# Block 1's pass of a graph network on one Trainium2 core: its stores issued by another queue, part of its arithmetic on GpSimd, and the corrected sums of split nodes in a block of their own

## What is computed

```python
def block1(x, src, dst, W, b):          # 200000 pairs and 12500 loops
    msg = relu(concatenate([x[src], x[dst]], axis=-1) @ W.T + b)
    agg = segment_sum(msg, src, num_segments=12500)
    return relu(concatenate([x, agg], axis=-1) @ W.T + b)

h = maximum(layernorm(x), 0); x = x + block0(h, src, dst)     # 4 softmax heads over the nodes, sum over edges, elu
h = maximum(layernorm(x), 0); x = x + block1(h, src, dst)
h = maximum(layernorm(x), 0); x = x + block2(h, src, dst)     # three graph attention layers: 8, 8 and 1 heads
h = maximum(layernorm(x), 0); x = x + block3(h, edge_attr)    # a mean of messages over the edges
```

## Time and profile before

| | |
|---|---|
| median of 3 runs | 15976.06 us (15976.02 to 15996.48) |
| profiled execution | 15981.7 us, span 15980.0 us |
| busy, share of the span | TensorE 51%, VectorE 42%, ScalarE 35%, GpSimd 70% |
| phase e1, first to last copy of sums | about 5076 to 5820 us |
| phases f0 and f1 | 2399 to 2445 us and 5824 to 5870 us |

### The profile page before, as it was taken

The page is one execution under the profiler, slowest core; times in us unless marked ns, Lnnn a source line. Parts: engine busy times, 40 slices in busy tenths (PEclk is TensorE's granted clock), DMA queues, the critical chain, the costliest instruction groups (busy, mean ns, idle before and its releaser), DMA issues. The chain is left out here.

```text
span 15980.0 us, 259817 instructions
## 1 busy us (share of the span) xinstructions
PE 8190.7 (51%) x75456; PEld 7411.3 (46%) x75456; DVE 6692.7 (42%) x24144; ACT 5666.0 (35%) x13371; POOL 11257.5 (70%) x11862
## 2 busy tenths in 40 slices
PE   6555552565664763434432444432344444888886
PEld 4555441455554653333332333332344443777775
DVE  5555554777775863333335333335222224211112
ACT  2555551677774531222221222221111112333332
POOL 4777767677775457777767777776777775577776
PEclk9776765878877975666665666665555555799998
DMA  4444442222223743444432444443333332344443
GB/s 153 162 161 162 162 142 57 96 93 91 92 93 120 257 155 93 146 146 146 146 117 72 146 146 146 146 143 60 77 85 85 85 85 54 119 146 146 146 146 97
DMA packets 895395, 1965.03 MB, mean 123 GB/s; under 512 B 392230, under 2 KB 471026, under 8 KB 854067
## 3 DMA queue, kind: packets, MB, share of 16 engines
q0 software_dynamic: 361120, 582.27, 15.9%
q1 hardware_dynamic: 426179, 797.11, 14.6%
q10 hardware_dynamic: 107776, 582.40, 9.5%
HBM read 1095.74 MB, written 894.54 MB: 125 GB/s over the span
## 5 line engine op out<-in xcount | busy, mean ns | idle before, releaser
L112 POOL DMA_INDIRECT eg_got<-gat_table,eg_rows x4992 | 4714.7, 944 | 1542.1 <-issue 1512.5
L112 POOL DMA_INDIRECT e_got<-table,e_rows x3328 | 3155.6, 948 | 1031.2 <-issue 1004.6
L1321 PE MATMUL eg_ps_sum<-eg_got,eg_equal 128*128 128x136 f32 (+1 forms) x9984 | 2070.8, 382 | 280.3 <-DVE eg_got L1409 256.5
L1328 ACT ACTIVATE eg_outs<-eg_ps_sum 128x544 f32<-128x544 f32 (+1 forms) x1248 | 675.1, 541 | 4279.2 <-PE eg_ps_sum L1321 4268.9
L1321 PEld LDWEIGHTS eg_ps_sum<-eg_got,eg_equal 128*128 128x128 f32 x9984 | 1965.5, 291 | 344.2 <-ACT eg_outs L1328 189.1
L117 POOL DMA_INDIRECT sorted_rows<-sort_rows,sort_dest x1664 | 1615.9, 971 | 532.8 <-issue 495.9
L1353 PE MATMUL eg_small<-ident,eg_score 128*128 128x128 f32 (+1 forms) x312 | 138.6, 444 | 3176.1 <-DVE eg_score L1392 3176.1
L1353 PEld LDWEIGHTS eg_small<-ident,eg_score 128*128 128x128 f32 (+1 forms) x312 | 47.2, 151 | 3203.5 <-DVE eg_score L1392 3203.5
L1390 DVE TENSOR_TENSOR eg_diff<-eg_small,eg_got 128x128 f32<-128x128 f32 (+1 forms) x312 | 79.1, 253 | 2732.6 <-DMA eg_got<-gat_table,eg_rows 2732.6
L1621 DVE TENSOR_SCALAR e_got<-e_ps_second 128x512 f32<-128x512 f32 x416 | 287.6, 691 | 1758.0 <-PE e_ps_second L1604 1727.5
L567 PE MATMUL e_ps_sum<-e_got,e_equal 128*128 128x64 f32 x3328 | 628.8, 352 | 676.1 <-DMA e_got<-table,e_rows 676.1
(11 more groups left out here) (528 smaller groups left out, 20828.1 us busy)
## 6 DMA issues: line engine op xcount, KB each, us to landing
gat_out<-eg_outs ACTq DMA_DIRECT2D x208, 1152.0 KB
eg_equal_b<-equal_d SPq DMA_DIRECT2D x312, 512.0 KB
out<-e_outs ACTq DMA_DIRECT2D x208, 512.0 KB
out<-e_outs ACTq DMA_DIRECT2D x104, 1024.0 KB
values<-e_zeros_b SPq DMA_DIRECT2D x104, 768.0 KB
values_q<-e_zeros_b SPq DMA_DIRECT2D x104, 768.0 KB
sort_value<-values_q SPq DMA_DIRECT2D x104, 768.0 KB
e_value<-values SPq DMA_DIRECT2D x104, 768.0 KB
```

The source lines that it names most:

```text
L112: return e.indirect_dma_start(out, None, table, bass.IndirectOffsetOnAxis(ap=index, axis=0), **kw)
L1321: last_i = e.matmul(ps_sum[q % 2][:, i, 0:FG], equal[q % 4][:, i, :], got[k][:, t, :], start=True, stop=True)
L1328: e.activation(outs[k % 2][:, tiles, 0:FG], ps_sum[q % 2][:, :, 0:FG], ACT.Copy).then_inc(copied.sem, 1)
```

## The change

1. In e1 SP issues the stores of `out` and `last`. Its loop loads group k of the next turn, then stores group k of this turn; the first turn's loads stand ahead of the loop, the last turn's stores behind it, and `keys.load` behind those. There are four `outs` buffers instead of two.
2. In e1 the rests of odd quads go: ScalarE writes relu(rows) in fp32 to `rest` (a third activation for such a quad), GpSimd subtracts the first part from it in place. Even quads are left with VectorE. GpSimd's part stands at reach 3, before `third_part`.
3. `out` of each pass has 1664 more rows. `finish_sums` stores `patch` there in one DMA from SP. A node whose edges cross a tile has its `end_row` pointed at that block: row EP + (tile % 128) * 13 + tile / 128 for its last tile. That is worked out once at the end of e0, for both orders. `PatchRows`, `span`, `first_key`, `patch_row` and the 13 scatters of each of the six `finish_sums` are gone; `keys.load` carries one table instead of two.

The core of the diff:

```diff
@@ first_pass: VectorE's tables at the end of e0
-            e.tensor_copy(span[:, :, :, 0], pos[:, 0]).then_inc(ve, 1)
-            e.tensor_copy(span[:, :, :, 1], pos[:, 1]).then_inc(ve, 1)
+            e.tensor_scalar(tile_i[:, :, :, :], pos_i[:, :, :, :], 7, None, ALU.logical_shift_right).then_inc(ve, 1)
+            e.tensor_copy(tile_f[:, :, :, :], tile_i[:, :, :, :]).then_inc(ve, 1)
+            e.tensor_scalar(split_i[:, 0], tile_i[:, 1], P - 1, None, ALU.bitwise_and).then_inc(ve, 1)
+            e.tensor_scalar(split_i[:, 1], tile_i[:, 1], 7, None, ALU.logical_shift_right).then_inc(ve, 1)
+            e.tensor_tensor(crosses[:, :, :], tile_f[:, 0], tile_f[:, 1], ALU.not_equal).then_inc(ve, 1)
+            e.tensor_copy(split_f[:, :, :, :], split_i[:, :, :, :]).then_inc(ve, 1)
+            e.scalar_tensor_tensor(split_f[:, 0], split_f[:, 0], float(TB), split_f[:, 1], ALU.mult, ALU.add).then_inc(ve, 1)
...
+            e.scalar_tensor_tensor(split_f[:, 0], split_f[:, 0], float(EP), row_f[:, 1], ALU.add, ALU.subtract).then_inc(ve, 1)
+            e.tensor_tensor(split_f[:, 0], split_f[:, 0], crosses[:, :, :], ALU.mult).then_inc(ve, 1)
+            e.tensor_tensor(row_f[:, 1], row_f[:, 1], split_f[:, 0], ALU.add).then_inc(ve, 1)
@@ carried_pass
-        outs = [ph.sb(f"outs{k}", [P, GT, D]) for k in B2]
+        outs = [ph.sb(f"outs{k}", [P, GT, D]) for k in G4]
...
         def sync(e):
-            with e.Fori(0, TURNS) as it:
+            def load(it, k):
+                g = bass.ds(it * n4 + k, 1)
+                e.wait_ge(fills.sem, fills.at(it, (k + 1) * QUADS - U))
+                e.dma_start(value[k][:, :, :], values_v[g, :, :, :].rearrange("g p t c -> (g p) t c")).then_inc(loaded[k].sem, 16)
+                e.wait_ge(less_even.sem, less_even.at(it, ((k + 1) * QUADS - U) // 2))
+                e.wait_ge(cut_1.sem, cut_1.at(it, (k + 1) * QUADS - U))
+                e.dma_start(rows[k][:, :, :], rows_v[g, :, :, :].rearrange("g p t c -> (g p) t c")).then_inc(loaded[k].sem, 16)
+            def store(it, k):
+                g = bass.ds(it * n4 + k, 1)
+                e.wait_ge(copied.sem, copied.at(it, (k + 1) * QUADS))
+                e.dma_start(out_v[g, :, :, :].rearrange("g p t c -> (g p) t c"), outs[k][:, :, :]).then_inc(stored[k].sem, 16)
+                for a in B2:
+                    e.dma_start(ends_v[g, a, :, :], outs[k][a * (P - 1):a * (P - 1) + 1, :, :]).then_inc(stored[k].sem, 16)
+            for k in G4:
+                load(0, k)
+            with e.Fori(0, TURNS - 1) as it:
                 for k in G4:
...
+                    load(it + 1, k)
+                    store(it, k)
+            for k in G4:
+                store(TURNS - 1, k)
             keys.load(e)
+            for k in G4:
+                e.wait_ge(stored[k].sem, stored[k].at(0, TURNS))
...
-            stepped(e, (3, rests), (5, add), (7, compare))
+            stepped(e, (3, even_rests), (5, add), (7, compare))
...
             def first_part(it, q):
                 e.wait_ge(summed.sem, summed.at(it, q + 1 - CUTS))
+                if q % 2:
+                    e.wait_ge(cut_3.sem, cut_3.at(it, q + 1 - n4))
+                    e.activation(rest[q % 4][:, :, :], rows[k][:, tiles, 1:], ACT.Relu).then_inc(relued.sem, 1)
                 e.activation(cut[q % CUTS][:, 0], rows[k][:, tiles, 1:], ACT.Relu).then_inc(cut_1.sem, 1)
...
+            def odd_rests(it, q):
+                if q % 2:
+                    e.wait_ge(relued.sem, relued.at(it, q // 2 + 1))
+                    e.wait_ge(cut_1.sem, cut_1.at(it, q + 1))
+                    e.tensor_tensor(rest[q % 4][:, :, :], rest[q % 4][:, :, :], cut[q % CUTS][:, 0], ALU.subtract).then_inc(less_odd.sem, 1)
-            stepped(e, (1, third_part))
+            stepped(e, (3, odd_rests), (1, third_part))
@@ finish_sums
+            e.wait_ge(patched, 1)
+            e.dma_start(out[EP:EP + T].rearrange("(q b) c -> q b c", b=TB), patch[:, :, :]).then_inc(patch_out, 16)
+            e.wait_ge(patch_out, 16)
...
-            for b in range(TB):
-                scatter(e, out[:, :], self.patch_row[:, s, b:b + 1], patch[:, b, :], EP - 1).then_inc(patch_out, 16)
@@ Collect
-                gather(e, self.to[:, t, :], self.out[:, :], self.end_row[:, t:t + 1], EP - 1).then_inc(self.rows_in[j], 16)
+                gather(e, self.to[:, t, :], self.out[:, :], self.end_row[:, t:t + 1], EP + T - 1).then_inc(self.rows_in[j], 16)
```

More of the change, by code:

```diff
@@ L350, in first_pass @@
         pos_i = ph.sb("pos_i", [P, 2, 2, P], I32)
-        span = ph.sb("span", [P, 2, P, 2], I32)
+        tile_i = ph.sb("tile_i", [P, 2, 2, P], I32)
+        tile_f = ph.sb("tile_f", [P, 2, 2, P])
+        split_i = ph.sb("split_i", [P, 2, 2, P], I32)
+        split_f = ph.sb("split_f", [P, 2, 2, P])
+        crosses = ph.sb("crosses", [P, 2, P])
         node_rows = ph.sb("node_rows", [P, 2, 2, P], I32)
@@ L361, in first_pass @@
         group_in = ph.sem("group_in")
-        self.span = [self.dram(f"span{s}", (NP, 2), I32) for s in B2]
         row_tab = self.dram("row_tab", (2, 2, NP), I32)
@@ L1070, in carried_pass @@
         loaded = [Tally(ph, f"loaded{k}", 1, 32) for k in G4]
-        stored = [Tally(ph, f"stored{k}", 2, 48, ahead=16) for k in B2]
+        stored = [Tally(ph, f"stored{k}", 1, 48, ahead=48) for k in G4]
         spread = Tally(ph, "spread", U)
@@ L1075, in carried_pass @@
         added = Tally(ph, "added", U, ahead=2)
-        cut_1 = Tally(ph, "cut_1", U)
-        less = Tally(ph, "less", U, ahead=U)
+        cut_1 = Tally(ph, "cut_1", U, ahead=U)
+        relued = Tally(ph, "relued", U // 2)
+        less_even = Tally(ph, "less_even", U // 2, ahead=U // 2)
+        less_odd = Tally(ph, "less_odd", U // 2)
         cut_2 = Tally(ph, "cut_2", U)
@@ L1157, in add, with even_rests @@
                 e.tensor_tensor(rows[k][:, tiles, 1:], ps_fill[q % 2][:, :, 0:D], rows[k][:, tiles, 1:], ALU.add).then_inc(added.sem, 1)
-            def rests(it, q):
-                k, tiles, _ = place(q)
-                e.wait_ge(cut_1.sem, cut_1.at(it, q + 1))
-                e.wait_ge(cut_3.sem, cut_3.at(it, q + 1 - n4))
-                e.scalar_tensor_tensor(rest[q % 4][:, :, :], rows[k][:, tiles, 1:], 0.0, cut[q % CUTS][:, 0], ALU.max, ALU.subtract).then_inc(less.sem, 1)
+            def even_rests(it, q):
+                if q % 2 == 0:
+                    k, tiles, _ = place(q)
+                    e.wait_ge(cut_1.sem, cut_1.at(it, q + 1))
+                    e.wait_ge(cut_3.sem, cut_3.at(it, q + 1 - n4))
+                    e.scalar_tensor_tensor(rest[q % 4][:, :, :], rows[k][:, tiles, 1:], 0.0, cut[q % CUTS][:, 0],
+                                           ALU.max, ALU.subtract).then_inc(less_even.sem, 1)
             e.wait_ge(group_in, 16)
@@ L1745, in finish_sums @@
             ins = [(acc_t, slice(0, FO), FO)]
-            patch_rows = PatchRows(self, ph, s) if name in ("f0", "f1") else None
         F = HF if heads else FO
@@ L1878, in vector @@
             e.sem_inc(patched, 1)
-        ph.run(sync=sync, gpsimd=gpsimd, tensor=tensor, vector=vector, scalar=scalar)
+        ph.run(sync=sync, gpsimd=gpsimd if heads else None, tensor=tensor, vector=vector, scalar=scalar)
     def block0(self):
@@ L2060, in block0 @@
         self.sort()
-        out = self.dram("out0", (EP, D))
+        out = self.dram("out0", (EP + T, D))
         last = self.dram("last0", (2, T, D))
@@ L2171, in block1 @@
         values = self.values1
-        out, last = self.dram("out1", (EP, D)), self.dram("last1", (2, T, D))
+        out, last = self.dram("out1", (EP + T, D)), self.dram("last1", (2, T, D))
         self.carried_pass(values, out, last)
@@ L2231, in gat_layer @@
         FG, FO = HF + heads, HF + 2 * heads
-        out, last = self.dram(f"gat_out{n}", (EP, FO)), self.dram(f"gat_last{n}", (2, T, FO))
+        out, last = self.dram(f"gat_out{n}", (EP + T, FO)), self.dram(f"gat_last{n}", (2, T, FO))
         self.gat_pass(f"eg{n}", table, out, last, self.values2, heads, ch)
@@ L2433, in block23 @@
         ph.run(sync=sync, gpsimd=close.collect.gpsimd, tensor=tensor, vector=vector, scalar=scalar)
-        out, last = self.dram("out3", (EP, H)), self.dram("last3", (2, T, H))
+        out, last = self.dram("out3", (EP + T, H)), self.dram("last3", (2, T, H))
         self.attr_pass("e3", table, out, last, (w_attr, w_mid, b_rows, one_rows), (w_own, w_right, w_left, w_c_t, w_join, bias_e))
@@ L2873, in __init__ @@
     def __init__(self, kn, ph, s, table, dt):
-        self.first_key, self.to, self.table, self.ints = kn.first_key[s], kn.links[:, s, :], table, dt is I32
-        self.by_tile, self.last = ph.sb("key_by_tile", [NG, 2, GT], dt), ph.sb("key_last", [P, T], dt)
+        self.to, self.table, self.ints = kn.links[:, s, :], table, dt is I32
+        self.by_tile, self.last = ph.sb("key_by_tile", [NG, GT], dt), ph.sb("key_last", [P, T], dt)
```

(2 more changed lines are left out.)

126 lines of the change are left out of this document (34 added, 92 removed).

## The result

| | before | after |
|---|---|---|
| median of 4 runs each | 15976.56 us (15976.02 to 15996.48) | 15680.63 us (15680.12 to 15693.26) |
| profiled execution, its span | 15981.7, 15980.0 us | 15693.3, 15691.1 us |
| first to last copy of sums in e1 (415 quads on) | 5080.3 to 5819.9 us, 739.6 | 5054.2 to 5608.5 us, 554.3 |

The ratio is 0.9814 with the interval 0.9803 to 0.9826: 296 us less by the medians, 289 us by the two spans.

A forecast was written before the change was run, and what follows sets the result against it. No engine was full; e1 was taken to be paced by ScalarE's store issuing. Terms -181 (e1), -57 and -64 (`finish_sums`), +13.5 (key tables), +3 (e0) sum to -285.5: 15976 to 15690 us, range 15640 to 15760.

The forecast's parts named there:

- What bounds the kernel: In e1, ScalarE's issuing of three stores stops the engines together once a group, 1.53 of 7.14 us.
- Rival 3: e1 stays at 7.14 us a group because another wait replaces the stop: 15871 us, chance 0.05.
- Parts 1 to 3: e1: stores to SP, odd rests to GpSimd, DMAs become the floor; 7.14 to 5.4 us a group, 181 us saved.
- Part 2: e1: odd rests by GpSimd relieve VectorE, whose group then takes 5.0 to 5.65 us with port waits.
- Part 4: End of e1: `keys.load`, now behind the last store, comes out from under cover; +13.5 us (+10 to +16).
- Parts 5 and 6: Ends of six `finish_sums`: one store replaces 13 scatters; -57 us in f0 and f1, -64 in the four others.
- Part 7: End of e0: ten operations added to the row numbers, two casts and two DMA issues removed; +3 us.
- Rival 1: e1: GpSimd keeps the port, a waiting rest lets two queued instructions pass; 5.75 us a group, 15726 us, chance 0.22.
- Rival 2: e1: the DMA floor is softer, TensorE and VectorE hold 5.05 us a group; 15654 us, chance 0.12.
- Rival 4: e1 slower: value load waits in SP behind the store, group goes to 8.45 us; some 16020 us, chance 0.03.
- the list of what would be wrong: TensorE waiting for loads of `rows` or `value` in e1, or a store of corrected sums taking over 7 us.
- part 3: e1: the DMAs become the floor, 5.2 us a group, against 5.05 us of the engines' cadence.

The follow-up runs named there:

- e0: A phase of the kernel, not a run; ten operations on the row numbers were added at its end, measured +2.2 us.
- sp_stores: Kernel before the change, with only e1's stores moved to SP and four output buffers: 15818.12 us against 15989.31, ratio 0.9893.
- act_four_outs: Kernel before the change with four output buffers instead of two, stores still on ScalarE: 740.1 us from first to last copy in e1, against 739.6.
- odd_rests: Kernel before the change, with only the odd quads' rests moved to GpSimd and ScalarE's extra activation: 15943.18 us, ratio 0.997.
- half_value: Changed kernel loading only 8 of 16 value tiles per group after e1's first turn: 15641.2 us, ratio 0.9782 to the kernel before.
- more_loads: Changed kernel with 384 KB more loaded per group into a buffer nothing reads: 597 us from first to last copy in e1, 5.75 us a group.
- keys_early: Changed kernel with `keys.load` moved ahead of e1's pass: 3.97 us from last copy to f1's first DMA, against 12.7; first to last copy 553.4 us.

## Why the prediction was right, step by step

**What bounds the kernel: right.** The 1.53 us of issuing set the pace. sp_stores shows it by taking it away alone, act_four_outs by leaving it and changing the buffers. The sentence that VectorE's 1.26 us is the cadence between the stops is right too; odd_rests shows it, as it gains 0.45 us a group. Rival 3 is refuted by the 171 us of sp_stores. The Trainium skill (DMA: Bandwidth & Descriptors, section "Issuing engines are not separate DMA queues") calls the sequencer's time for issuing usually small beside the DMA; in this loop it was 1.53 us at the stop shown and 1.65 in the mean, of 7.13. What the prediction did not have is the clock: the echo of the stop in the kernel before includes stretches at the lower clock in 24 of 99 groups (7.44 us for 7.12), and the changed kernel has none. As an estimate from these, they are 8 of the 185 us.

**Parts 1 to 3, 5.4 us a group: right, 5.34 measured, -185.3 for -181.** But the mechanism was right only in part, and some luck is in the closeness. The two ends of the range, DMA 5.2 and VectorE waiting 5.6, were not both at work. That the transfers hold the pass is shown by half_value and by TensorE's wait for `rows`. The step "not below 5.2", a floor of full occupation, is wrong: it took a busy share of 0.98 at 348 GB/s in one burst as all that the DMA engines can do. At the 388 GB/s of more_loads the same 1808 KB would take 4.8 us, less than the engines' 4.88, and 2192 KB went in 5.75. For VectorE waiting for the port I expected half to all of 0.63 us for an even rest. Its mean over the pass, and its shortest, middle and longest duration in ns:

```profile
L1199 DVE SCALAR_TENSOR_TENSOR e_rest<-e_rows,e_cut 128x256 f32<-128x256 f32 x207 | 129.0, 623 | 32.9 <-ACT e_cut L1218 32.5
...
L1199 DVE SCALAR_TENSOR_TENSOR e_rest<-e_rows,e_cut x208: 410/611/809, 5049.5 to 5603.4; 128x256 f32<-128x256 f32 x104
```

0.62 against 0.41 undisturbed is 0.21 us, a third of it. VectorE still has 31 of 400 us idle, so little of it can have reached the end of the pass; no run takes it away. Part 2 is worth 1 to 7 of 185 us.

**Part 4: the mechanism right, the size too large.** +8.8 for +13.5, outside the +10 to +16 given. The chain took 12.7 us for 17.4. Two terms make most of it: the load by tile, which I took at 5 us between 3.3 and 7.07, is 3.24 (5609.93 to 5613.17), and the write with one issue is 1.33, not 2.9. Both were taken from rows in which the pass's own transfers ran beside them. sp_stores parts the two reasons: without those transfers a pair of loads took 4.45 instead of 7.07, and one load 3.24; a pair of writes 1.76 instead of 3.26, and one 1.33. So the company of the pass cost 2.6 and 1.5 us, and the second DMA of a pair 1.2 and 0.4. The store issues, the broadcast (4.3 for 4.8) and the change of phase are each 0.4 to 0.5 us below their terms.

**Parts 5 and 6: right.** -57.3 for -57; -66.0 for -64, as the end of an attention layer took 4.7 us for the 5.4. The bound of -102 for parts 5 and 6 together is a slip: six ends at 7.1 us instead of the 27.7 in all that the two parts use give -106. **Part 7:** +2.2 for +3; the operations on 256 elements follow each other every 0.46 us, within the 0.2 to 0.47 taken.

**Rival 1** (GpSimd keeps the port, even rests over 1.2 us) is refuted: at 5304.55 the rest got in between two queued `third_part`, and no even rest of the pass took longer than 0.81 us. **Rival 2** (the floor softer, 5.05) is refuted in its result, 75 loads in 400 us and not 79, though its idea was right: more_loads and the 407 and 422 GB/s of loads alone and the store alone show a softer floor. **Rival 4** (the value load waits behind the store) needed a landing of 14 us. The value load does stand behind the store now, and the 51st load of `rows`, issued at 5300.62, is waited for until 5308.97, 8.35 us. Of the list of what would be wrong, one thing came: TensorE waits for the load of `rows`. By part 3, in which the DMAs are the floor, it had to come, so the prediction contradicted itself there.

**What stays open** is which property of the transfers holds 5.34 us. Within one group of the changed kernel the windows differ:

```profile
5303.00:5306.50 3.50, 3.48 (x84) 3.17 (x80) 3.50 (x9) 3.15 (x12) 2.88 (x5) 1.00 1.00 391
5306.50:5308.50 2.00, 1.63 (x44) 1.50 (x40) 2.00 (x5) 1.85 (x7) 1.78 (x4) 1.00 0.87 275
```

Over 100 us of quarter-microsecond windows a third of the time (0.33) is below 330 GB/s, with a mean of 260; in more_loads 0.15. The groups are uneven too: from one store of `out` to the next they take 4.85 to 6.07 us, where half_value has 4.78 to 4.94. Averaged over 56 groups, the rate is some 375 GB/s in the two us behind the issue of a store, falls to 230 at 3.0 to 3.5 us behind it and is back by 4.75. In half_value it falls to 30 at 2.5 us behind the store, so almost nothing was under way there. One reading was that stores go at a lower rate than loads; the 422 GB/s of the last store speaks against it. Another is the landing: a buffer of `rows` that is free by the reaches at about the time of the store's wait (5303.88) is refilled only from 5306.08, behind three stores and a value load in SP's queue, and then needs, if it lands like the load of 5300.62, 8.35 us of the four groups' 21.4. The once-a-group fall fits this reading but doesn't show it. By it, loads issued ahead of the stores, or the load of `rows` ahead of that of `value`, would bring something. Neither was tried.

## What to carry to other kernels

An engine's queue that issues DMAs between its instructions stops for the time of issuing; where the engine is a link in a round trip, as ScalarE here with 1.53 us a group, that time is on the path though the engine is half idle, and it shows as idle "issue". An idle time can also cost the clock behind it: here TensorE went to the lower level for some 3 us after some of its stops. Change one cause and ask what holds next before spending work on the second: here the transfers came next, and relieving VectorE brought 1 to 7 us of the 15.5 us that it is worth with half of the value load gone. Small steps that used to run under a pass (the key tables) come out when they are queued behind its last instruction, and may go ahead of it, as keys_early did for 8.7 us less at the end and about 1 more at the start. A price read from rows under load is too high for the same step in a quiet queue.

## What was not expected of the hardware

- The DMA rate is no constant of the pass: 345 GB/s with 1808 KB a group, 298 with 1424 (held by the engines), 388 with 2192, all from one queue on SP. Loads alone ran at 407 for 12 us. The Trainium skill (HBM Reference, section "Specifications (TRN2)") gives a core some 358 GB/s, and well above that, about 425, when it streams alone; 388 and 407 lie above the first and below the second, on a program that uses one core.
- The DMA share can exceed 1 (1.01 in more_loads), so a share of 0.96 did not mean that no more bytes would fit.
- VectorE and GpSimd instructions with two SBUF inputs each took turns also when GpSimd's next instruction was ready: at 5304.55 0.54 us for a rest and 1.49 for two third parts, instead of 0.41 and 2 x 0.67.
- A chain of small DMAs depends more on what runs beside it than on their number: a pair of loads by tile took 7.07 us under the pass and 4.45 behind it, one alone 3.24; a pair of writes to DRAM 3.26 and 1.76, one 1.33.
- TensorE's clock fell after work had begun again, not during the stop: in odd_rests the granted clock was 1.00 while TensorE stood idle up to 5162.87, and 0.50 from 5163.50 to 5166.50 with TensorE fully busy.
